# Softmax attention with split exponentials: the full exponentials go back into PSUM over the scores, and VectorE alone takes the low parts

## The reference

```python
scores = jnp.einsum('bhqd,bhkd->bhqk', q, k) * scale      # scale = 1/8, 2048 queries x 2048 keys, 32 (batch, head) pairs
attn = jax.nn.softmax(scores, axis=-1)
out = jnp.einsum('bhqk,bhkd->bhqd', attn, v)
```

## Time and profile before

| what | value |
|---|---|
| three runs | 4502.37, 4507.91, 4509.51 us (median 4507.91) |
| the profiled execution | 4506.27 us |
| its span, first to last instruction | 4504.5 us |
| mean granted clock of TensorE | 0.931 |
| TensorE, VectorE, ScalarE, GpSimd busy, share of span | 88%, 79%, 59%, 49% |

### The profile page before, as it was taken

How to read it: one execution, slowest core, us unless ns; L and a number is a source line. 1 busy time by engine, 2 the same in 40 slices (tenths; PEclk the granted TensorE clock), 3 DMA queues, 4 the chain that set the end, 5 groups by cost and what they waited for, 6 DMA issues and landing times. The chain is left out here.

```text
span 4504.5 us, 54711 instructions
## 1 busy us (share of the span) xinstructions
PE 3984.1 (88%) x17866; PEld 3005.5 (67%) x17866; DVE 3574.9 (79%) x4436; ACT 2646.0 (59%) x3555; POOL 2209.0 (49%) x1837
## 2 busy tenths in 40 slices
PE   6774998683999999999999999999999999989563
PEld 3443554452788888888888888888888888867421
DVE  4454443774899999999999999999999999956611
ACT  4442333331677777777777777777777777742221
POOL 1234665464455555555555555555555555530154
PEclk8776999786999999999999999999999999989776
DMA  6001333666222232223222322232223223137296
GB/s 242 20 22 39 56 61 59 221 217 185 63 53 57 49 81 50 57 49 81 53 53 49 81 55 53 57 76 56 51 58 72 56 51 64 34 113 235 74 243 165
DMA packets 349678, 384.04 MB, mean 85 GB/s; under 512 B 141532, under 2 KB 279585, under 8 KB 336851
## 3 DMA queue, kind: packets, MB, share of 16 engines
q1 hardware_dynamic: 325334, 354.22, 30.8%
q0 software_dynamic: 24064, 26.32, 3.5%
HBM read 232.55 MB, written 117.84 MB: 78 GB/s over the span
## 5 line engine op out<-in xcount | busy, mean ns | idle before, releaser
L1523 POOL TENSOR_TENSOR at_pl<-at_pf,at_ph 128x512 fp32r<-128x512 f32 x1024 | 1330.0, 1299 | 1343.0 <-ACT at_ph L1670 1342.7
L1669 ACT ACTIVATE at_pf<-at_ps_s 128x1024 f32<-128x1024 f32 x1024 | 1051.0, 1026 | 747.5 <-PE at_ps_s L1719 747.5
L1586 DVE TENSOR_TENSOR at_pl<-at_pf,at_ph 128x512 fp32r<-128x512 f32 x1024 | 1355.4, 1324 | 20.6 <-ACT at_ph L1670 20.6
L1568 DVE TENSOR_REDUCE at_mx<-at_ps_u 128x2 f32<-128x1024 f32 x1024 | 1250.2, 1221 | 24.5 <-PE at_ps_u L1703 24.4
L1670 ACT ACTIVATE at_ph<-at_ps_s 128x1024 fp32r<-128x1024 f32 x1024 | 1042.7, 1018 | 0.0
L1719 PE MATMUL at_ps_s<-at_q,at_k 66*128 66x512 f32 x2048 | 820.7, 401 | 0.0
L1718 PE MATMUL at_ps_s<-at_q,at_k 128*128 128x512 f32 x2048 | 812.2, 397 | 0.3 <-ACT at_ph L1670 0.3
L1735 PE MATMUL at_ps_v<-at_ph,at_vh 128*128 128x512 f32 x2048 | 810.1, 396 | 0.2 <-POOL at_pl L1523 0.2
L1737 PE MATMUL at_ps_v<-at_pl,at_vh 128*128 128x512 f32 x2048 | 809.5, 395 | 0.0
L1736 PE MATMUL at_ps_v<-at_ph,at_vl 128*128 128x512 f32 x2048 | 809.2, 395 | 0.0
L1703 PE MATMUL at_ps_u<-at_k,at_qp 128*128 128x512 f32 x2048 | 648.0, 398 | 63.5 <-DMA at_q<-at_low 47.7
(11 more groups left out here) (254 smaller groups left out, 4116.1 us busy)
## 6 DMA issues: line engine op xcount, KB each, us to landing
at_k<-kT SPq DMA_DIRECT2D x64, 512.0 KB, 10.0
at_q<-qT SPq DMA_DIRECT2D x64, 512.0 KB, 9.3
wgu<-Wgu_in SPq DMA_DIRECT2D x64, 384.0 KB, 5.2
qT<-pj_rot SPq DMA_DIRECT2D x32, 512.0 KB, 3.1
vT<-pj_vo SPq DMA_DIRECT2D x32, 512.0 KB, 4.4
kT<-pj_rot SPq DMA_DIRECT2D x32, 512.0 KB, 3.1
at_raw<-qT SPq DMA_DIRECT2D x32, 512.0 KB, 4.7
at_raw<-kT SPq DMA_DIRECT2D x32, 512.0 KB, 6.6
```

What stands on the lines that cost most here:

```text
L1523: pool.tensor_tensor(pl[:, n % NP, at], pf[:, n % NP, at], ph[:, n % NP, at].bitcast(F32), ALU.subtract).then_inc(s["pl2_ready"], 1)
L1568: dve.tensor_reduce(mx[:, qb % 2, 2 * i:2 * i + 2], ps_u[:], X, ALU.max).then_inc(s["u_max"], 1)
L1586: dve.tensor_tensor(pl[:, n % NP, at], pf[:, n % NP, at], ph[:, n % NP, at].bitcast(F32), ALU.subtract)\
L1669: act.activation(pf[:, n % NP], ps_s[:, n % 2], ACT.Exp, scale=DH ** -0.5)
```

## The change

ScalarE now computes `ph` first. It then waits until that instruction has ended and computes the full exponentials in place, `ps_s` to `ps_s`, raising a new semaphore `pf_ready`. The SBUF tile `pf` is gone. VectorE takes the low part of the whole slot, 128 x 1024, with one operand in PSUM and one in SBUF. GpSimd keeps only the splits of the values. TensorE's `scores(n + 2)` now waits for `pl_ready` of slot n in place of `p_ready`, since the slot's scores are read last by VectorE.

```diff
@@ GpSimd @@
-                def low_part(g, n):
-                    pool.wait_ge(s["p_ready"], g * SLOTS + (n + 3))
-                    stand_alone(pool, s["turns"])
-                    at = slice(QB, 2 * QB)
-                    pool.tensor_tensor(pl[:, n % NP, at], pf[:, n % NP, at], ph[:, n % NP, at].bitcast(F32),
-                                       ALU.subtract).then_inc(s["pl2_ready"], 1)
...
                     for n in range(SLOTS):
-                        if n + 1 < SLOTS or prepare:
-                            low_part(g, n + 1)
                         i = n - SLOTS // 2
@@ VectorE @@
                 def low_part(g, n):
-                    dve.wait_ge(s["p_ready"], g * SLOTS + (n + 3))
-                    at = slice(0, QB)
-                    dve.tensor_tensor(pl[:, n % NP, at], pf[:, n % NP, at], ph[:, n % NP, at].bitcast(F32), ALU.subtract)\
+                    dve.wait_ge(s["p_ready"], g * SLOTS + (n + 1))
+                    dve.wait_ge(s["pf_ready"], g * SLOTS + (n + 1))
+                    if n >= NP or not isinstance(g, int) or g > 0:
+                        dve.wait_ge(s["pv_done"], g * SLOTS + (n + 1))
+                    dve.tensor_tensor(pl[:, n % NP], ps_s[:, n % 2], ph[:, n % NP].bitcast(F32), ALU.subtract)\
                         .then_inc(s["pl_ready"], 1)
@@ ScalarE @@
                         act.wait_ge(s["pv_done"], pr * (2 * SLOTS) + (n + 1))
-                        act.activation(pf[:, n % NP], ps_s[:, n % 2], ACT.Exp, scale=DH ** -0.5)
                         act.activation(ph[:, n % NP], ps_s[:, n % 2], ACT.Exp, scale=DH ** -0.5)\
                             .then_inc(s["p_ready"], 1)
+                        act.wait_ge(s["p_ready"], pr * (2 * SLOTS) + (n + 1))
+                        act.activation(ps_s[:, n % 2], ps_s[:, n % 2], ACT.Exp, scale=DH ** -0.5)\
+                            .then_inc(s["pf_ready"], 1)
@@ TensorE, scores @@
                     if j == 0:
-                        pe.wait_ge(s["p_ready"], g * SLOTS + (n + 1))
+                        if g > 0 or n > 1:
+                            pe.wait_ge(s["pl_ready"], g * SLOTS + (n - 1))
@@ TensorE, values @@
                         pe.wait_ge(s["pl_ready"], g * SLOTS + (n + 1))
-                    else:
-                        pe.wait_ge(s["pl2_ready"], g * SLOTS + (n + 1))
```

More of the change, by code:

```diff
@@ L1377, in softmax_attention @@
             nml = sb("nml", [P, NQB, NQB], F32R)
-            pf = sb("pf", [P, NP, 2 * QB])
             ph = sb("ph", [P, NP, 2 * QB], F32R)
@@ L1389, in softmax_attention @@
             names = ("turns raw0 raw1 kq0 kq1 v0 v1 fixed own cut_ready low_ready low0 low1 qp_ready u_full u_max mg_ready nm_ready "
-                     "row0 row1 row2 row3 s_full p_ready pl_ready pl2_ready vh_ready v_split pv_done "
+                     "row0 row1 row2 row3 s_full p_ready pf_ready pl_ready vh_ready v_split pv_done "
                      "o_ready o0_out o1_out den recip rden").split()
@@ L1540, in _ @@
                     low_values(0, 0, i)
-                low_part(0, 0)
                 for pr in range(PAIRS - 1):
@@ L1643, in _ @@
                 act.sem_inc(s["pv_done"], NP)
-                act.sem_inc(s["p_ready"], 2)
                 act.sem_inc(s["o_ready"], 2)
```

## The result

The changed kernel takes 4520.3 us (median of 10 runs, 4516.35 to 4528.26) and the kernel before 4503.99 us on the same chip: ratio 1.0037, interval 1.0027 to 1.0047. It is 16 us slower. The profiled execution of the changed kernel has a span of 4522.7 us at a mean granted clock of 0.932. Of the executions of the kernel before that stand beside the last two experiments, two at 5243 and 9662 us, with granted clocks of 0.72 and 0.41, are left out; every other one lies at 0.929 to 0.935.

The account below looks back on a forecast made before the run. TensorE was taken to bound the kernel; stalls 9.0, start 1.4 and 1.0, and end 0.2 sum to +11.6 us on 4506.3 us, giving a forecast of 4518 us, range 4504 to 4570 us.

Parts of the forecast that it names:

- The bound: TensorE bounds the attention at 2.80 us a slot; removing GpSimd's low parts is by itself worth 0.
- rival 4: Without GpSimd's SBUF traffic matmuls run faster; decides from 0.001 us a matmul, 4481 us at 0.003 less; chance 0.05.
- The chain: Scores through ScalarE and VectorE's low part back to TensorE: 4.54 us against two slots of 5.60, 1.06 to spare.
- Rival 3: In-place exponential slow on shared PSUM banks, deciding from 1.45 us: 4555 us at 1.6, 4926 at 2.06; chance 0.10.
- The walk: VectorE's order from slot 9: cuts, take_low and stabilisers exceed 0.90 us of cover, stalling slot 13 by 0.29 us a head.
- Rival 1: VectorE's crowded iterations 9 to 11 cost nothing as the cover just holds: 4508 us, no change; chance 0.22.
- rival 2: Dearer waits or stabilisers stall iterations 2, 18 and 26 too, +37 to +62 us, 4545 to 4568 us; chance 0.13.
- Stalls: One TensorE stall of 0.29 us in each of 31 heads with a next head, +9.0 us.
- Start: At slot 0 the longer chain delays TensorE by 1.4 us, and a later clock rise adds 1.0.
- the clock's 1.0: At the start a longer gap may delay TensorE's rise to the upper clock level: 0 to 2.4 us, taken as +1.0.
- End: The last slot waits for a chain longer by a few tenths, +0.2 us.
- the likeliest: One short stall a head, 0.1 to 0.5 us, giving 4511 to 4528 us; chance 0.50.

Follow-up runs that it names:

- the last two experiments: e6_wait_alone, and a kernel releasing scores by ScalarE with full exponentials in SBUF, odd products of the start going to ps_v, 4489.15 us.
- e4_release: Changed kernel with full exponentials in SBUF and TensorE's scores waiting for ScalarE's second exponential instead of VectorE's low part: 4507.04 us, ratio 1.0000.
- e3_sbuf: Changed kernel with full exponentials written to SBUF tile pf and the low part reading pf, TensorE's wait unchanged: 4524.27 us, ratio 1.0039.
- e1_spread: Changed kernel with VectorE's four cuts a head in iterations 4, 6, 12 and 14 instead of 7, 9, 11 and 13: 4511.07 us, ratio 1.0010.
- e6_wait_alone: Kernel before, low parts still halved between VectorE and GpSimd, but TensorE's scores wait for both halves: 4552.97 us, ratio 1.0107.

## Why the prediction was right

**The bound.** TensorE sets the pace in plain slots after the change too: 2.80 us a slot, now with VectorE waiting for it. GpSimd's 1330 us of low parts were worth nothing by themselves, as e4_release shows: without them, and without the new wait, the time is the old one within 0.1%. Plain slots are 2.7988 us after and 2.7999 before, so rival 4, a faster matmul, is out too: it is 0.0001 us a matmul, where it needed 0.001 to decide.

**The chain.** The unknown costs came out at the values taken. The self-wait is 0.02 us (1141.98 + 1.03 to 1143.03), the in-place exponential 1.01 for 1.03, the low part 1.22, ScalarE to VectorE 0.10 for 0.03; VectorE now has two waits there in place of one, but no run shows that this is why. Rival 3, the dear exponential, is out, by the row and by e3_sbuf. From the low part to the next instruction it is 1.13 us in the rows above (2347.44 to 2348.57). The estimate of 1.19 us from the section on the TRN2 errata in "VectorE: DVE Perf Modes" of the Trainium skill is 0.06 us above this trace.

**The walk.** Place, size and cause of the stall are shown: slot 13, once a head, 0.29 us, gone with the cuts moved, grown as walked with the cuts crowded. Rival 1 missed by those 0.29 us, rival 2 did not happen in the steady heads: iterations 2, 18 and 26 kept their cover, but for four single slots. All four stand behind stabilisers: slot 28 of head 3, slot 4 of head 11, slot 12 of head 20 and slot 20 of head 28. In the first three VectorE starts the low part 0.31, 0.30 and 0.17 us late, with "issue" as the reason; in the last it idles 0.48 us between lines 1562 and 1567 in place of 0.11. The timeline of the second:

```profile
2147.62 0.16 DVE L1569 SCALAR_TENSOR_TENSOR at_nml<-at_mg,at_nmh 128x4 fp32r<-128x4 f32 x1
...
2148.08 1.22 DVE L1577 TENSOR_TENSOR at_pl<-at_ps_s,at_ph 128x1024 fp32r<-128x1024 f32 x1 [0.30 <-issue]
...
2149.36 0.50 PE L1711 MATMUL at_ps_s<-at_q,at_k 128*128 128x512 f32 x1
```

What makes VectorE issue late there stays open, but it is no accident of one execution: the same slots of the same heads are late in e1_spread and e3_sbuf. The traces of before and of e6_wait_alone have such gaps at three other places, the same in both (0.46 us twice between stabilisers, 0.2 once), and there TensorE didn't wait for them.

**The terms that were too small.** The sum was 11.6 us against 16.3 by the medians and 16.2 in the attention's own stretch. Stalls: 9.0 forecast, 13.2 measured, of which 31 x 0.11 = 3.4 us is TensorE's restart. The sum let TensorE go on from the moment the semaphore is up, but the weights of the first matmul, otherwise loaded ahead of it, are then loaded in the open. The four single slots add 1.1 us, which the sum had at nothing. The reciprocal of head 17 (0.8 us) was overlooked, though its code stands in the same loop. Start: 2.4 forecast, 2.15 measured, of which the chain's 1.4 was right (1.45) and the clock's 1.0 (0.7 here) could as well have been -0.5, as in e3_sbuf. End: 0.2 forecast, 0.8 measured. The median lies 2 us above the number given and within the range. That the number is so near is partly luck: the change was forecast 4.7 us too small, but the kernel before came out at 4503.99 us, 2.3 under the 4506.3 that the sum began from. Of the cases, the likeliest came true, in its slower half.

## What to carry to other kernels

Before a buffer's release is moved from one engine to a later one, walk the later engine's program through its most crowded stretch, not through its average slot: VectorE was 90% busy (359.63 of 400 us from 1800 to 2200) and still 0.29 us late once in 32 slots, and that was most of the loss. The remedy is then order (spread the extras: most of the loss went, without a new instruction) or an earlier release (ScalarE's, which gave all of it back, and which needs the full exponentials in SBUF). Add TensorE's restart, 0.11 us here, to each wait that it newly meets, and remember that work taken from another engine buys nothing unless the engine that sets the pace waited for it.

## What was not expected of the hardware

- A wait that holds TensorE's matmul up costs more than its length. Behind it the first matmul of 512 columns lasts 0.50 in place of 0.39 us and the slot is 0.11 us longer. A weight load held up by 0.17 us at slot 12 cost nothing.
- ScalarE reading and writing the same two PSUM banks takes 1009 ns for 1024 columns, less than into SBUF (1026 ns in e3_sbuf).
- GpSimd's splits run much faster beside the new low part, which reads one operand from PSUM: the page of before gives 844 ns for the cast and 1056 ns for the subtraction; the groups of after from 1500 to 3700 us give 396 and 739 ns. In e3_sbuf, where the low part reads both operands from SBUF, they take 645 and 1145 ns. So what VectorE reads beside them counts here. The groups of after:

```profile
L1515 POOL TENSOR_TENSOR at_vl<-at_vf,at_vh 128x256 fp32r<-128x256 f32 x100 | 73.9, 739 | 18.3 <-POOL at_vh L1509 18.3
...
L1509 POOL CAST at_vh<-at_vf 128x256 fp32r<-128x256 f32 x100 | 39.6, 396 | 2122.9 <-PE at_ps_v L1728 1866.0 <-DMA at_vf<-vT 256.9
```
